# A fused attention and expert kernel: two routing tables for three, wide head sums, an earlier first image, and a new order of work

## The chip, the cores and the metric

One core of a Trainium2 chip runs the whole program in one launch. The metric is the device time of one execution in microseconds (us). Times inside the program are counted from its first instruction. The engines have names of their own in what follows: TensorE (PE, and PEld for its weight loads), VectorE (DVE), ScalarE (ACT), GpSimd (POOL) and SyncE (SP), which here only issues transfers.

## The reference, cut to what matters

Eight images of 128 channels and 256 positions go through three layers; T = 2 halves of 128 positions make an image.

```python
# 1. per image: self-attention over positions, with a key mask
sim = softmax((wq x + bq)^T (wk x + bk) / 8 + key_mask);  x = x + gamma * (sim @ (wv x))
# 2. t = tokens of x.  L = 256, but the sequence axis of this layer is the 8 images:
q, k = relu(LN(t) @ q_w.T + q_b), relu(LN(t) @ k_w.T + k_b);  v = LN(t) @ v_w.T + v_b
q_, k_ = [q*sin, q*cos], [k*sin, k*cos]              # angle by the position in the sequence
attn = (q_ @ cumsum(k_ v)) / max(q_ @ cumsum(k_), eps)   # causal, 8 heads of 16
t = t + attn @ out_w.T + out_b
# 3. mixture of 8 experts, the best 2 per token
probs = softmax(LN(t) @ router_w); w, e = top_k(probs, 2); w = w / w.sum()
t = t + sum over the 2 of  w * (silu(x @ w1[e]) * (x @ w3[e])) @ w2[e]
```

The causal sum over images is written out: for image i and every earlier or equal image j, the product of q(i) and k(j), summed within each head and times the cosine of the gap i - j, is the weight of v(j).

## The kernel before, in words

Each engine runs a list of steps, written out by hand in its own order; semaphores tie them together. The lists are the long rows of calls at the end of each engine's function. A step is a small function with the same name on every engine's side of the work, and its number is the image or the block.

- **Conv layer** (`conv_...`, per image): projections (L646, L647, L653), scores (L661), row maxima on VectorE (L899), exponentials on ACT (L529), turns by TensorE (L671), the product with the values (L681).
- **Linear layer** (`lin_...`, per image i): a norm whose root is taken on GpSimd (L455), projections (L698, L699, L705), products q(i) k(j) for all j <= i on VectorE (L951), the **head sums** on TensorE in `lin_scores` (L720): the product is the stationary operand, and a [128, 8] slice of the constants (the cosine in the rows of each head) is the moving one, so that every matmul moves 8 columns. Then VectorE weights (L974), values (L989), turns that add over j (L733) and the output projection `lin_out` (L743, L744). Images from the third on have products and values in two halves.
- **Routing** (`route_...`, per image): norm, logits (L758), the two best, ranks by triangular matmuls (L770 to L776), a slot for each of the token's two rows. GpSimd scatters rows with four indirect DMAs per image (L474) into `rows_x` in DRAM, where each expert has room for all tokens. `rows_x` is first filled with blank rows from the tile `pad` by nine large DMAs on SyncE's queue (L411, L413).
- **Tables.** The 39 blocks of 128 rows are not known before routing. A table says for each block where its rows start and which expert it has. `PHASES` (L37) says when tables are made: after 4 images for 9 blocks, after 6 images for blocks up to 17, after all 8 for the rest. A table takes `count` and `t_turn` on TensorE and some ten small steps (`t_...`) on VectorE. SyncE waits for the table and for the scatters of its images before it loads the rows of its blocks (L418, L424).
- **Expert blocks.** Per block s: `turn_x` (L795), its copy on ACT (L584), `gate_up` (L809, four f32 matmuls, eight instructions), silu on ACT (L590), `hidden` on VectorE (L1183), `down` (L820), `weigh` (L1204), `store`, an indirect DMA of GpSimd into `rows_y` (L483). The weights of the expert are copied into a ring of three, by ACT (`weights`, L602) for blocks before the last table, by VectorE (L1194) for those of it.
- **End.** When all stores have landed, `rows_y` is read back in six parts, added to the tokens (L1265, L1267) and written out.

The queue of SyncE is in order: image 0 (X), WC, VEC, CF, XT of image 0, small constants, X and XT of the other images, the expert weights W13 and W2, then the blank fill. The first conv projection waits for both transfers of its image (L644), since they count on one semaphore. GpSimd clears `pad` first. The stores and the scatters share GpSimd's list: stores 0 to 3 stand before the scatters of images 6 and 7.

Of the kernel before, what the change touches and what calls it, by code (L numbers as in the profile page):

```python
# [15 lines left out]
P = 128  # L16
B = 8
# [5 lines left out]
H = 8  # L23
# [13 lines left out]
PHASES = ((4, 9), (6, 17), (B, BLOCKS),)  # L37
# [60 lines left out]
def hybrid_block(nc, x_ch, x_tok, w_conv, w_lin, w_router, w13, w2, vecs, bias_rows, cst_f, cst_tri, cst_dest,  # L98
                 out):
    ctx = ExitStack()  # L100
    with ctx:
# [15 lines left out]
        W13 = sb("W13", [P, E * 2 * F])  # L117
        W2 = sb("W2", [P, E * FK * P])
# [44 lines left out]
        num = sb("num", [P, 2, B, T * P])  # L163
        attT = sb("attT", [P, 2, N])
# [34 lines left out]
        pad = sb("pad", [P, CAP // P, ROW])  # L199
# [47 lines left out]
        ld_x = [sem(f"ld_x{i}") for i in range(B)]  # L247
        ld_vec = sem("ld_vec")
# [34 lines left out]
        qk_done = sem("qk_done")  # L283
        sc_done = sem("sc_done")
# [106 lines left out]
        def _(sp):  # L391
            sp.dma_start(X[:, 0, :], x_ch[:, 0, :]).then_inc(ld_x[0], 16)
            sp.dma_start(WC[:, :], w_conv).then_inc(ld_conv, 16)
            sp.dma_start(VEC[:, :], vecs).then_inc(ld_vec, 16)
            sp.dma_start(CF[:, :], cst_f).then_inc(ld_cst, 16)
            sp.dma_start(XT[:, 0, :, :], x_tok[:, 0, :, :]).then_inc(ld_x[0], 16)
# [16 lines left out]
            sp.dma_start(rows_x[DUMMY:DUMMY + P, :], pad[:, 0, :]).then_inc(rows_blank, 16)  # L413

# [27 lines left out]
        def _(pool):  # L442

            pool.memset(pad[:, :, 0:DEST_COL], 0.0).then_inc(pad_ready, 1)
            pool.memset(pad[:, :, DEST_COL:ROW].bitcast(I32), SKIP).then_inc(pad_ready, 1)
            pool.wait_ge(ld_dest, 16)
# [40 lines left out]
            rstd_lin(0); rstd_lin(1); rstd_lin(2); rstd_ffn(0); rstd_ffn(1); rstd_lin(3); rstd_lin(4); scatter(0, 0)  # L487
            scatter(0, 1); scatter(0, 2); scatter(0, 3); rstd_ffn(2); rstd_lin(5); scatter(1, 0); scatter(1, 1)
            scatter(1, 2); scatter(1, 3); rstd_lin(6); rstd_ffn(3); rstd_lin(7); scatter(2, 0); scatter(2, 1)
            scatter(2, 2); scatter(2, 3); scatter(3, 0); scatter(3, 1); scatter(3, 2); scatter(3, 3); rstd_ffn(4)  # L490
            rstd_ffn(5); scatter(4, 0); scatter(4, 1); scatter(4, 2); scatter(4, 3); rstd_ffn(6); scatter(5, 0)
            scatter(5, 1); scatter(5, 2); scatter(5, 3); store(0); rstd_ffn(7); store(1); store(2); store(3)
            scatter(6, 0); scatter(6, 1); scatter(6, 2); scatter(6, 3); scatter(7, 0); scatter(7, 1); scatter(7, 2)
            scatter(7, 3)
            for s in range(4, BLOCKS):
                store(s)

        @block.scalar
        def _(act):

            act.wait_ge(ld_vec, 16)
# [126 lines left out]
            for s in range(16, 38):  # L628
                turn_and_silu(s)

        @block.tensor
        def _(pe):
# [76 lines left out]
            def lin_scores(i, share):  # L709
# [5 lines left out]
                if share == 0:  # L715
                    bank_free(BANK_SC, sco_done, i + 1)
# [141 lines left out]
            for s in range(13, BLOCKS + 1):  # L858
                block_step(s)
# [454 lines left out]
```

## Time and profile before

| what | value |
|---|---|
| median of 3 runs | 211.65 us (210.78 to 212.57) |
| the profiled execution | 212.31 us, of which its span is 210.2 us |
| PE busy | 161.9 us, 77% of the span |
| PE weight loads | 148.7 us, 71% |
| DVE busy | 117.7 us, 56% |
| ACT busy | 75.7 us, 36% |
| POOL busy | 89.5 us, 43% |
| mean granted clock of TensorE | 0.875 |

### The profile page before, as it was taken

Reading aid. Unit: us, or ns where it says so; the run is one execution under the profiler, and the core shown is the slowest. Engines: PE = TensorE matmul, PEld = TensorE weight load, DVE = VectorE, ACT = ScalarE, POOL = GpSimd, SP = SyncE. Lnnn points to the kernel's source line nnn. Section 1 sums busy time; section 2 is a strip of 40 time slices with the busy share of each in tenths; the row PEclk is TensorE's granted clock in tenths of the full one; section 3 lists DMA queues with packets and bytes.
Section 4 is the critical chain, followed back from the end, with each engine's and each line's share of the span. In section 5 each row is a group of like instructions: output and inputs, shape, how many; then the busy total and the mean of one; then the engine's idle time right before and its main releaser. Section 6 shows DMA issues by size and latency. Waiting matters only on the chain.

```text
span 210.2 us, 4168 instructions
## 1 busy us (share of the span) xinstructions
PE 161.9 (77%) x1161; PEld 148.7 (71%) x1161; DVE 117.7 (56%) x475; ACT 75.7 (36%) x227; POOL 89.5 (43%) x94
## 2 busy tenths in 40 slices
PE   0998999999499998899997885731999899992000
PEld 0677888989499887799996875731999888881000
DVE  0525566888559888655453853412465555553154
ACT  2256767563471530021451553304242333330000
POOL 4001111215862267502756543774476556657000
PEclk9999999999969998555589699996699999999555
DMA  5789999950110001113101024111443220110395
GB/s 127 213 257 382 427 420 411 422 224 13 40 54 0 0 28 41 38 30 87 38 26 54 22 69 102 41 50 37 101 112 107 71 73 21 35 47 0 111 278 210
DMA packets 15475, 25.33 MB, mean 121 GB/s; under 512 B 3083, under 2 KB 13008, under 8 KB 14174
## 3 DMA queue, kind: packets, MB, share of 16 engines
q1 hardware_dynamic: 13182, 20.84, 29.7%
q0 software_dynamic: 2272, 4.24, 6.2%
q8 instruction: 10, 0.16, 0.3%
q14 instruction: 11, 0.09, 0.1%
HBM read 10.67 MB, written 14.85 MB: 121 GB/s over the span
## 4 chain that ended last, share of the span: by engine, by line
PE 67%; another core or an unknown queue 8%; issue 5%; DMA 5%; ACT 5%; DVE 3%; SPq 2%; POOL 1%; POOLq 1%; ACTq 1%; DVEq 0%
PE ps L809 18%; PE ps L720 7%; PE ps L820 7%; PE ps L733 5%; PE ps L681 4%; PE ps L661 4%; PE ps L743 3%; DMA num<-rows_y 3%; PE ps L795 2%; PE ps L671 2%; PE ps L698 2%; PE ps L699 2%; PE ps L646 2%; PE ps L705 2%
## 5 line engine op out<-in xcount | busy, mean ns | idle before, releaser
L483 POOL DMA_INDIRECT rows_y<-yb,xb x39 | 39.5, 1012 | 23.7 <-DVE yb L1204 14.7
L809 PE MATMUL ps<-xbT,WB 128*128 128x128 f32 x312 | 46.5, 297 | 2.5 <-issue 2.4
L809 PEld LDWEIGHTS ps<-xbT,WB 128*128 128x128 f32 x312 | 42.4, 211 | 3.8 <-issue 3.8
L474 POOL DMA_INDIRECT rows_x<-xrow,slot x32 | 34.3, 1071 | 24.2 <-DVE slot L1085 16.2
L1204 DVE TENSOR_SCALAR yb<-ps,xb 128x128 f32<-128x128 f32 x39 | 13.6, 348 | 39.3 <-PE ps L820 23.5
L590 ACT ACTIVATE gate<-ps 128x256 f32<-128x256 f32 x39 | 14.9, 384 | 41.2 <-PE ps L809 28.7
L820 PE MATMUL ps<-W,hid 128*128 x156 | 25.0, 285 | 1.1 <-DVE hid L1183 1.1
L795 PE MATMUL ps<-CF,xb 128*128 128x128 f32 x39 | 11.8, 303 | 14.4 <-ACT xbT L584 11.2
L820 PEld LDWEIGHTS ps<-W,hid 128*128 128x128 f32 x156 | 21.4, 199 | 1.7 <-issue 1.5
L720 PEld LDWEIGHTS ps<-CF,qk 128*128 128x128 f32 x144 | 20.4, 223 | 0.2
L720 PE MATMUL ps<-CF,qk 128*128 128x8 f32 x144 | 20.4, 275 | 0.0
L455 POOL TENSOR_TENSOR rs<-ve,CF 128x2 f32<-128x2 f32 x8 | 6.7, 843 | 28.9 <-DVE ve L933 28.9
L795 PEld LDWEIGHTS ps<-CF,xb 128*128 128x128 f32 x39 | 6.3, 160 | 15.4 <-issue 15.2
L1183 DVE TENSOR_TENSOR hid<-gate,ps 128x256 f32<-128x256 f32 x39 | 16.1, 412 | 1.0 <-ACT gate L590 1.0
L461 POOL TENSOR_TENSOR rs<-ve,CF 128x2 f32<-128x2 f32 x8 | 6.6, 826 | 22.4 <-DVE ve L1015 21.9
L584 ACT ACTIVATE xbT<-ps 128x128 f32<-128x128 f32 x39 | 10.8, 278 | 13.3 <-PE ps L795 6.1
L733 PE MATMUL ps<-CF,num 128*128 128x128 f32 x72 | 14.0, 350 | 0.9 <-DVE num L989 0.9
L951 DVE TENSOR_TENSOR qk<-kT,qT 128x768 f32<-128x768 f32 (+3 forms) x13 | 11.6, 892 | 2.1 <-ACT kT L549 1.7
L733 PEld LDWEIGHTS ps<-CF,num 128*128 128x128 f32 x72 | 11.5, 185 | 1.8 <-DVE num L989 0.9
L989 DVE TENSOR_TENSOR num<-vt,sco 128x768 f32<-128x768 f32 (+3 forms) x13 | 11.6, 891 | 0.5 <-DVE sco L974 0.3
L602 ACT ACTIVATE WB<-W 128x512 f32 x17 | 10.6, 626 | 2.6 <-DVE table L1160 2.0
L681 PE MATMUL ps<-cv,probT 128*128 128x128 f32 x64 | 8.8, 281 | 2.8 <-ACT cv L520 2.8
(128 smaller groups left out, 286.9 us busy)
## 6 DMA issues: line engine op xcount, KB each, us to landing
rows_x<-pad SPq DMA_DIRECT2D x8, 1105.0 KB, 21.5
xb<-rows_x SPq DMA_DIRECT2D x39, 65.0 KB, 1.9
W<-in_w SPq DMA_DIRECT2D x1, 2048.0 KB, 10.3
num<-rows_y SPq DMA_DIRECT2D x8, 192.0 KB, 4.6
X<-in_x_ch SPq DMA_DIRECT2D x8, 128.0 KB, 3.2
XT<-in_x_tok SPq DMA_DIRECT2D x8, 128.0 KB, 3.6
W<-in_w SPq DMA_DIRECT2D x1, 1024.0 KB, 12.2
out_tok<-num SPq DMA_DIRECT2D x4, 192.0 KB, 3.6
```

Source lines behind the costliest of these rows:

```text
L474: pool.indirect_dma_start(rows_x, bass.IndirectOffsetOnAxis(ap=slot[:, g:g + 1], axis=0), xrow[:, g // TOP_K, g % TOP_K, :], None, bounds_ ...
L483: pool.indirect_dma_start(rows_y, bass.IndirectOffsetOnAxis(ap=xb[:, n, DEST_COL:ROW].bitcast(I32), axis=0), yb[:, n, :], None, bounds_che ...
L590: act.activation(gate[:, s % GATE, :], ps_gu[s % 3][:, 0:F], ACT.Silu).then_inc(gate_done, 1)
L681: last = pe.matmul(ps_co[:, t, :], probT[:, b, k, t * P:(t + 1) * P], cv[:, b, k, :], start=(k == 0), stop=(k == T - 1))
L720: last = pe.matmul(ps_sc[:, j, t * H:(t + 1) * H], qk[:, i % 2, j, t * P:(t + 1) * P], heads, start=True, stop=True)
L733: last = pe.matmul(ps_aT[:, t * P:(t + 1) * P], num[:, i % 2, j, t * P:(t + 1) * P], ident, start=(j == 0 and t == 0), stop=(j == i), is_t ...
L795: pe.transpose(bank(xbT_bank(s))[:, 0:P], xb[:, s % RING, 0:P], ident).then_inc(xbT_done, 1)
L809: last = pe.matmul(ps_gu[s % 3][:, k * P:(k + 1) * P], WB[:, s % WBS, k * P:(k + 1) * P], xbT[:, s % XBT, :], start=True, stop=True)
L820: last = pe.matmul(ps_yb[s % 2], hid[:, s % HID, k * P:(k + 1) * P], W2[:, bass.ds(experts[s] * (FK * P) + k * P, P)], start=(k == 0), sto ...
L951: dv.tensor_tensor(qk[:, i % 2, first:end, :], kT[:, first:end, :], qT[:, i % 2, :].unsqueeze(1).broadcast_to([P, end - first, N]), ALU.mult)\
L1183: dv.tensor_tensor(hid[:, s % HID, :], gate[:, s % GATE, :], ps_gu[s % 3][:, F:2 * F], ALU.mult)\
L1204: dv.tensor_scalar(yb[:, n, :], ps_yb[s % 2], xb[:, n, W_COL:W_COL + 1], None, ALU.mult).then_inc(yb_done, 1)
```

## The change

`PHASES` becomes two tables: 13 blocks after 5 images, and the other 26 after all 8. ACT copies the weights of blocks 0 to 12 and VectorE those of 13 to 38.

The head sums get a moving operand of 128 columns. `HZ` holds, for every gap, the 8 cosine columns with zeros on both sides; a slice of it puts the 8 columns where image j and half t have theirs, and all matmuls of an image add up in the same 128 columns of PSUM.

The weights of the conv layer and VEC are issued by ACT. XT of image 0 gets a semaphore of its own. The expert weights come behind the blank fill and wait for it, since `pad` is now a view of the first 2,210 columns of W13. GpSimd also clears HZ and copies the cosines into it. TensorE starts with 22 bf16 matmuls of 128 columns on the tile ONES. The lists of all engines are in a new order; on GpSimd all scatters now stand before the first store.

```diff
-PHASES = ((4, 9), (6, 17), (B, BLOCKS),)
+PHASES = ((5, 13), (B, BLOCKS),)
...
+        pad = W13[:, 0:CAP // P * ROW].rearrange("p (k d) -> p k d", d=ROW)
+        HZ = sb("HZ", [P, B, (2 * B * T - 1) * H])
-        pad = sb("pad", [P, CAP // P, ROW])
...
             sp.dma_start(X[:, 0, :], x_ch[:, 0, :]).then_inc(ld_x[0], 16)
-            sp.dma_start(WC[:, :], w_conv).then_inc(ld_conv, 16)
-            sp.dma_start(VEC[:, :], vecs).then_inc(ld_vec, 16)
             sp.dma_start(CF[:, :], cst_f).then_inc(ld_cst, 16)
-            sp.dma_start(XT[:, 0, :, :], x_tok[:, 0, :, :]).then_inc(ld_x[0], 16)
+            sp.dma_start(XT[:, 0, :, :], x_tok[:, 0, :, :]).then_inc(ld_xt0, 16)
...
-            sp.dma_start(W13[:, :], w13).then_inc(ld_w13, 16)
-            sp.dma_start(W2[:, :], w2).then_inc(ld_w13, 16)
 
             sp.wait_ge(pad_ready, 2)
...
             sp.dma_start(rows_x[DUMMY:DUMMY + P, :], pad[:, 0, :]).then_inc(rows_blank, 16)
+
+            sp.wait_ge(rows_blank, 16 * (E + 1))
+            sp.dma_start(W13[:, :], w13).then_inc(ld_w13, 16)
+            sp.dma_start(W2[:, :], w2).then_inc(ld_w13, 16)
...
             pool.memset(pad[:, :, DEST_COL:ROW].bitcast(I32), SKIP).then_inc(pad_ready, 1)
+            pool.memset(HZ[:, :, :], 0.0).then_inc(heads_ready, 1)
+            pool.wait_ge(heads_ready, 1)
+            pool.wait_ge(ld_cst, 16)
+            pool.tensor_copy(HZ[:, :, (B * T - 1) * H:B * T * H],
+                             CF[:, C_COS:C_COS + B * H].rearrange("p (g h) -> p g h", g=B)).then_inc(heads_ready, 1)
...
-            scatter(5, 1); scatter(5, 2); scatter(5, 3); store(0); rstd_ffn(7); store(1); store(2); store(3)
-            scatter(6, 0); scatter(6, 1); scatter(6, 2); scatter(6, 3); scatter(7, 0); scatter(7, 1); scatter(7, 2)
-            scatter(7, 3)
-            for s in range(4, BLOCKS):
+            rstd_ffn(7); scatter(5, 0); scatter(5, 1); scatter(5, 2); scatter(5, 3); scatter(6, 0); scatter(6, 1)
+            scatter(6, 2); scatter(6, 3); scatter(7, 0); scatter(7, 1); scatter(7, 2); scatter(7, 3)
+            for s in range(0, BLOCKS):
                 store(s)
...
+            act.dma_start(WC[:, :], w_conv).then_inc(ld_conv, 16)
+            act.dma_start(VEC[:, :], vecs).then_inc(ld_vec, 16)
             act.wait_ge(ld_vec, 16)
...
+            def warm_up():
+
+                pe.wait_ge(dve, 1)
+                for _ in range(22):
+                    pe.matmul(ps_aT[:, 0:P], ONES[:, :], ONES[:, :], start=True, stop=True)
+
             def conv_proj_qk(i):
...
-                pe.wait_ge(ld_x[i], 32)
+                pe.wait_ge(ld_x[i], 32 if i else 16)
...
+                if i == 0:
+                    pe.wait_ge(heads_ready, 2)
                 for j in range(first, end):
-                    heads = CF[:, C_COS + (i - j) * H:C_COS + (i - j + 1) * H]
                     for t in range(T):
-                        last = pe.matmul(ps_sc[:, j, t * H:(t + 1) * H], qk[:, i % 2, j, t * P:(t + 1) * P], heads,
-                                         start=True, stop=True)
+                        at = (B * T - 1 - (j * T + t)) * H
+                        last = pe.matmul(ps_sc, qk[:, i % 2, j, t * P:(t + 1) * P], HZ[:, i - j, at:at + B * T * H],
+                                         start=(j == 0 and t == 0), stop=(j == i and t == T - 1), skip_group_check=True)
...
+            lin_proj_v(7); lin_out_turn(5, 0); route_turn(4); lin_scores(6, 0); route_logits(4); lin_scores(6, 1)
+            lin_out_turn(5, 1); lin_out(5); route_rank(4); count(0); lin_scores(7, 0); lin_scores(7, 1)
+            lin_out_turn(6, 0); lin_out_turn(6, 1); t_turn(0); lin_out(6); lin_out_turn(7, 0); route_turn(5)
+            route_logits(5); lin_out_turn(7, 1); turn_x(0); lin_out(7); turn_x(1); gate_up(0); turn_x(2); gate_up(1)
+            route_rank(5); route_turn(6); turn_x(3); gate_up(2); route_logits(6); down(0); route_turn(7); turn_x(4)
+            gate_up(3); down(1); route_rank(6); turn_x(5); gate_up(4); down(2); turn_x(6); route_logits(7)
+            gate_up(5); down(3); turn_x(7); gate_up(6); down(4); route_rank(7); count(1); turn_x(8); gate_up(7)
+            down(5); turn_x(9); gate_up(8); down(6); turn_x(10); t_turn(1); gate_up(9); down(7)
+            for s in range(9, BLOCKS + 1):
                 block_step(s)
...
-            dv.memset(ONES[:, :], 1.0)
+            link(dv.memset(ONES[:, :], 1.0))
...
-                dv.wait_ge(ld_x[i], 32)
+                dv.wait_ge(ld_xt0, 16) if i == 0 else dv.wait_ge(ld_x[i], 32)
```

## Rows read from the trace of the kernel before

**Rows 1.** Page: TensorE's granted clock in tenths, 40 equal slices.

```profile
PEclk9999999999969998555589699996699999999555
```

**Rows 2.** Stretches: length, busy us (instructions) by engine, granted clock, DMA share, GB/s.

```profile
0.00:14.20 14.20, 8.77 (x26) 6.32 (x27) 4.08 (x18) 5.29 (x13) 2.56 (x7) 1.00 0.74 197
14.20:58.60 44.40, 40.57 (x303) 36.15 (x302) 30.87 (x139) 26.41 (x80) 12.46 (x15) 1.00 0.71 286
58.60:62.00 3.40, 3.40 (x16) 3.12 (x15) 2.57 (x9) 2.24 (x5) 2.79 (x3) 0.51 0.15 44
62.00:82.50 20.50, 19.56 (x172) 18.51 (x171) 17.27 (x72) 6.83 (x21) 8.65 (x10) 1.00 0.06 18
82.50:106.40 23.90, 22.90 (x113) 21.56 (x112) 14.72 (x66) 5.78 (x18) 10.69 (x10) 0.50 0.18 48
106.40:116.60 10.20, 7.85 (x74) 7.42 (x73) 4.36 (x21) 3.96 (x12) 5.40 (x6) 1.00 0.11 34
116.60:120.00 3.40, 3.40 (x18) 3.40 (x18) 3.13 (x25) 2.10 (x7) 2.55 (x3) 0.51 0.07 22
120.00:143.90 23.90, 14.04 (x122) 12.74 (x121) 7.98 (x40) 7.99 (x23) 14.66 (x16) 1.00 0.24 65
143.90:150.70 6.80, 4.38 (x21) 4.41 (x22) 2.07 (x8) 1.90 (x6) 2.73 (x4) 0.50 0.22 56
150.70:188.50 37.80, 35.22 (x303) 33.78 (x303) 22.60 (x66) 12.59 (x44) 23.15 (x23) 1.00 0.26 69
```

**Rows 3.** Order of time, start: start us, us, engine, operation, idle before.

```profile
0.82 0.17 DVE L872 MEMSET ONES<- 65x128 bf16 x1 [0.82 <-PEq L1306]
...
5.20 1.09 PE L646 MATMUL ps<-X,WC 128*65 128x256 f32 x2 [5.20 <-DMA XT<-in_x_tok]
```

**Rows 4.** Chain that ended last: start us, us on the chain, what.

```profile
2.58 2.48 DMA XT<-in_x_tok
...
23.43 0.43 PE ps L699 x2
...
70.79 1.24 PE ps L720 x12
...
155.95 0.89 PE ps L809 x8
```

**Rows 5.** Order of time, around two holes, one long sum, one slow block.

```profile
57.13 1.13 PE L681 MATMUL ps<-cv,probT 128*128 128x128 f32 x8 [2.76 <-ACT cv L520]
...
78.65 3.27 PE L720 MATMUL ps<-CF,qk 128*128 128x8 f32 x28
...
133.82 1.06 PE L809 MATMUL ps<-xbT,WB 128*128 128x128 f32 x8
...
142.32 0.38 ACT L590 ACTIVATE gate<-ps 128x256 f32<-128x256 f32 x1 [4.73 <-remote]
...
145.87 0.35 DVE L1204 TENSOR_SCALAR yb<-ps,xb 128x128 f32<-128x128 f32 x1 [8.61 <-remote]
...
146.32 0.45 PE L795 MATMUL ps<-CF,xb 128*128 128x128 f32 x1 [6.58 <-ACT xbT L584]
...
149.14 0.42 PE L795 MATMUL ps<-CF,xb 128*128 128x128 f32 x1
```

**Rows 6.** Order of time, GpSimd: first and last of six stores back to back.

```profile
136.64 0.97 POOL L483 DMA_INDIRECT rows_y<-yb,xb  x1 [0.31 <-issue]
...
143.02 0.97 POOL L483 DMA_INDIRECT rows_y<-yb,xb  x1 [0.30 <-issue]
```

**Rows 7.** Groups by line: operation, shapes, count, busy us, mean ns, idle before.

```profile
L444 POOL MEMSET pad<- 128x2193 f32 x1 | 1.9, 1927 | 0.3 <-POOLq L1306 0.3
...
L706 PEld LDWEIGHTS ps<-BIAS,ONES 65*128 65x128 bf16 x16 | 1.6, 100 | 0.0
```

**Rows 8.** Stretches, line L809 alone: length, PE and PEld busy (instructions), clock, DMA.

```profile
82.50:106.40 23.90, 3.83 (x16) 3.69 (x16) 0.50 0.18 48
...
150.70:190.80 40.10, 25.09 (x187) 22.49 (x186) 1.00 0.25 67
```

More of the change, by code:

```diff
@@ L283, in hybrid_block @@
         qk_done = sem("qk_done")
+        heads_ready = sem("heads_ready")
         sc_done = sem("sc_done")
@@ new lines, in _ @@
+            turned_x(2); silu(1); route_xT(6); weights(4); turned_x(3); silu(2); weights(5); turned_x(4)
+            route_xT(7); route_lean(6); silu(3); weights(6); turned_x(5); silu(4); weights(7); turned_x(6); silu(5)
+            weights(8); route_lean(7); turned_x(7); silu(6); weights(9); turned_x(8); silu(7); weights(10)
+            turned_x(9); silu(8); weights(11); turned_x(10); silu(9); weights(12); turned_x(11); silu(10)
+            turned_x(12); silu(11); turned_x(13); silu(12)
+            for s in range(12, 38):
@@ L857, in _ @@
-            down(9); turn_x(13); gate_up(12); down(10); turn_x(14); gate_up(13); t_turn(2); down(11)
-            for s in range(13, BLOCKS + 1):
+            conv_scores(1); conv_out(0); conv_proj_qk(2); conv_proj_v(2); conv_turn(1); conv_scores(2); conv_out(1)
+            lin_turn(0); conv_proj_qk(3); conv_proj_v(3); lin_proj_qk(0); lin_proj_v(0); conv_turn(2)
+            conv_scores(3); lin_turn(1); lin_scores(0, 0); conv_out(2); lin_proj_qk(1); conv_turn(3); conv_proj_v(4)
+            lin_out_turn(0, 0); lin_proj_v(1); conv_proj_qk(4); lin_scores(1, 0); lin_out(0); lin_turn(2)
@@ L1258, in _ @@
-            weigh(12); hidden(14); weights(17); weigh(13); hidden(15)
-            for s in range(15, BLOCKS + 1):
+            conv_max(0); conv_inverse(0); conv_max(1); conv_add(0); lin_stats(0); conv_inverse(1); lin_moments(0)
+            lin_eps(0); lin_norm(0); conv_max(2); conv_add(1); lin_stats(1); conv_inverse(2); lin_moments(1)
+            lin_eps(1); lin_norm(1); lin_products(0, 0); conv_max(3); lin_sum(0); lin_floor(0); lin_inverse(0)
+            lin_weights(0); conv_add(2); conv_inverse(3); lin_values(0, 0); lin_stats(2); lin_moments(2)
@@ new lines, in _ @@
+            route_slots(6); weigh(2); hidden(4); route_top(7); route_index(7); route_gap(7); route_mask(7)
+            route_seen(7); weigh(3); hidden(5); route_weights(7); weigh(4); route_where(7); t_blocks(1)
+            route_slots(7); hidden(6); t_sum(1); t_ends(1); t_delta(1); t_past(1); weigh(5); t_skip(1); hidden(7)
+            t_expert(1); t_row(1); weigh(6); hidden(8); t_read(1); weigh(7); hidden(9); weigh(8); hidden(10)
+            weights(13); weigh(9); hidden(11)
+            for s in range(11, BLOCKS + 1):
```

142 lines of the change are left out of this document (57 added, 85 removed).

## The prediction

> **What bounds the kernel now.** I read the page first, then one table of stretches cut where the granted clock changes, then the order of time in the stretches that look odd. The page has TensorE as the busiest engine, and its clock line dips [rows 1]. The table of stretches is the main view [rows 2]. Up to 58.6 us TensorE is nearly full (40.57 us busy of 44.4) and is the bound. From 62 to 82.5 it is full and VectorE nearly so (17.27 of 20.5). From 82.5 to 106.4 the granted clock is 0.50: TensorE is busy for 22.90 of 23.9 us, but at the lower level, 1.2 GHz, so it is the bound only because of its clock; VectorE has 14.72 us of work there. From 106.4 to 150.7 nothing is full: TensorE is busy for 29.67 us of 44.3, 7.8 us of that at the lower level. From 150.7 to 188.5 TensorE is full again (35.22 of 37.8) with the expert blocks alone, and 21.7 us follow it: last blocks, last stores, sum, output.
>
> Two things in these views matter. The first 14 us: the page grants 1.00 there, but two 256-column matmuls take 1.09 us at 5.2 us [rows 3] and 0.43 us later [rows 4], so the array runs at 1.2 GHz at first, whatever the clock column says. And the holes after 106.4: gate_up(12) is done at 134.88, yet the silu that waits for it starts at 142.32, and VectorE, which waits for a `down` from before that, at 145.87; TensorE meanwhile stands still for 6.58 us [rows 5]. In that time GpSimd runs indirect stores back to back, one per 1.28 us [rows 6]. Neither ACT nor VectorE has another reason to wait, so signals of TensorE seem to arrive late while GpSimd has a backlog. A smaller hole of this kind is the 2.76 us before 57.13 [rows 5].
>
> **The sum, part by part**, against the profiled execution: span 210.2 us, 212.3 us with what lies around it, 0.3% above the median of 211.65 us.
>
> Start. The first matmul waits until 5.20 us for the second transfer of image 0 (XT), which only VectorE needs [rows 3]. The change gives it a semaphore of its own and issues WC and VEC from ACT's queue, so TensorE could start once X and WC are there; XT's own transfer took 2.48 us [rows 4], X and WC are issued by 1.2 us now, so about 3.6 us. In front of it are now 22 warm-up matmuls, from about 1 us on, when ONES is set [rows 3]. Their price is not in the trace: 22 weight loads of 100 ns [rows 7] (2.2 us) from below, and half more for a slow clock; the first real matmul then starts at 4.4 us. That saves 0.8 us (between a loss of 1.3 and a gain of 1.6). The clock: 8.77 us of work lie before 14.2 us, all slow [rows 2]. If it rises some 4.4 us sooner, that work shrinks by 2.2 us; bounds 0 and 4.4. ACT's two DMA issues go ahead of a table load and cost nothing that waits. **Start: -3.0 us.**
>
> GpSimd. HZ is cleared: 1984 columns at the rate of 2193 in 1.93 us [rows 7], 1.75 us, plus a small copy. GpSimd is busy for 2.56 of the first 14.2 us [rows 2], so 0. `pad` is set before it, so the fill of rows does not wait for it.
>
> SyncE's queue. Two issues leave its front and two of weights leave the place before the fill, which so comes four issues sooner, without 3 MB ahead of it. The weights now wait for the whole fill, SyncE with them; behind it on that queue are only row loads, far later. The first weights are wanted near 90 us, and the queues are quiet long before (a DMA share of 0.06 from 62 to 82.5 [rows 2]). **0.**
>
> Stretch 14.2 to 62. It is TensorE's own work. The dip at 58.6 (3.40 us busy, slow) follows the 2.76 us hole. I take half of the hole's chance: -1.0 for it, -1.7 for the dip. **-2.7 us**, bounds 0 and -4.5. So what stood at 62 stands at 56.3.
>
> Head sums. Two matmul instructions per pair of image and half, 144 in all, now move 128 columns instead of 8. Twelve 8-column ones take 1.24 us, 103 ns each; 128-column ones of the same type take 0.89/8 = 111 ns [rows 4]. The weight load behind each sets the pace, so the columns are nearly free: 144 x 8 ns = +1.2 us while TensorE is the bound. The column price if nothing hid it: a 256-column one takes 0.43/2 = 215 ns, 104 ns more for 128 columns, so 120 columns x 144 is at most +14 us.
> The Trainium skill (TensorE: Matmul & The Clock Gate, Back-to-back issue gap) lets the gap follow the moving columns down to a floor of about 25 ns, 56 ns for 128; by it alone the widening would cost 31 ns x 144 = 4.5 us and the time would be about 195. The rows disagree: 8 columns take 103 ns here.
>
> Stretch 62 to 106.4 (44.4 us). The clock falls at 82.5, right behind a run of 28 matmuls of 8 columns [rows 5]. If wide sums hold it at 2.4 GHz, TensorE's work of the linear stage is 19.56 + (22.90 - 5.4)/2 = 28.3 us, +1 for the sums; the 5.4 are two expert blocks' gate-and-up (3.83 [rows 8]) and some 1.6 of turns. VectorE's is 17.27 + 14.72 = 32.0 us and barely shrinks. VectorE becomes the bound, at 95%: 34 us. **-10.4 us.** So the point that was 106.4 is at 90.3, and lin_out(7), the last matmul of this stage, ends 2.5 us later, at 93. It has done no expert block yet, where the kernel before had done two.
>
> First table, 13 blocks, and the routing of images 5 to 7 among them. TensorE needs 1.62 us per block (37.8 us, 187/8 = 23.4 blocks [rows 2, 8]) plus some 3.5 us of routing: 25 us without a hole. The kernel before did 39 - 2 - 23.4 = 13.6 blocks between 106.4 and 150.7, 44.3 us; without its own 2.5 us of lin_out, 41 for 13. One table less takes away one place where everything waits for routing, and all of images 5 to 7 are routed while the 13 blocks run; but twelve indirect stores of rows now follow one another on GpSimd, with all 39 of the block outputs behind them, and such runs went with the holes. I leave 6 of the 16 us: **31 us, to 124**.
>
> Second table: 26 blocks x 1.62 = 42 us, +1 for the first rows to land: **43 us, to 167**. ACT no longer copies weights in them, VectorE does for 26 instead of 22; 22.60 us busy in 37.8 leave room [rows 2]. GpSimd: the last scatter ends near 116, and 39 stores at 1.28 us end at 166, with the last block. No term of its own, but no slack either.
>
> End as before: **21.7 us** [rows 2], so span 188.7, and with the 2.1 around it **191 us**.
>
> **Rivals.**
> A, the forecast: the clock holds in the linear stage, holes stay in part. 191 us, own range 184 to 198. Chance 0.42.
> B, the clock falls again in the linear stage, because waits on VectorE or the transposes between the sums let it. Then the -10.4 is lost: 201 us. For it: VectorE is the bound there, so TensorE will pause. Against: the stretch from 14.2 to 58.6, with many transposes, is granted 1.00 throughout [rows 2]. Chance 0.20.
> C, the holes stay at full size, because GpSimd's row of 12 scatters and a backlog of 13 stores makes them. The 13 blocks take 41 us: 201; if the backlog also stops the first blocks of the second table, as six stores stopped TensorE for 6.58 us, 207. Self-limiting, since GpSimd runs dry when no block ends. Chance 0.17.
> D, the holes go entirely: 185, with VectorE denser 180. Chance 0.10.
> E, slower: holes in the second table send the clock to 1.2 GHz and it stays there. A slow block takes 149.14 - 146.32 = 2.82 us [rows 5], 1.2 more than a fast one. From 19 of the 26 on the kernel is slower than before; all 26 give 191 + 31 = 222. For it: two such dips stand after holes. Against: both ended after 3.4 and 6.8 us [rows 2]. Chance 0.07.
> F, the sums cost their columns: 191 + 14 = 205. Chance 0.04.
>
> **The numbers.** About 1% can be told from no change here. The likeliest case gives 191. The range reaches from D's near end into C: 181 to 206, leaving out E, the far end of C and of D. Faster by over 1%: A, B, D, F and nearly all of C, 0.89, less 0.03 for several losses together: 0.86. Within 1%: 0.05. Slower: E and such sums, 0.09.
>
> **What would show it.** Start: first real matmul near 4.4 us, fast ones well before 14. Linear stage: granted clock 1.00 where it is 0.50 from 82.5 on, L720's mean no higher than 300 ns, VectorE over 90% busy, last lin_out near 93 us. First table: 13 blocks in about 31 us, with the longest idle times of TensorE before a transpose of rows, released by ACT. Second table: 1.62 us per block; GpSimd's stores without a pause. I am wrong if the granted clock falls among the wide sums, or if the stretch of the second table costs over 2 us per block.

## The result: 200.46 us, faster by 5.7%; and the profile after

The changed kernel takes 200.46 us (median of 4 runs, 198.63 to 202.54) against 211.22 us of the kernel before (4 runs, 210.31 to 212.57). The ratio is 0.943, with a 95% interval of 0.934 to 0.951. (Ratios, here and below, compare undisturbed runs alone and so may differ from the quotient of two medians.) I had forecast 191 us with a range of 181 to 206: the sign and the range held, but of the 20.7 us that I had expected only 10.8 came.

The profiled execution of the changed kernel is one of its longest, 202.54 us with a span of 200.4. So the sums below, which are made against that span, show some 2 us more than a typical execution has.

The page's row of the granted clock, 40 equal slices:

```profile
PEclk9999999999999999996698899855999999998555
```

The long low stretch of [rows 1], slices 17 to 20 (82.5 to 106.4 us in [rows 2]), is gone. What is left are dips behind 91 us. The table of stretches, cut where the clock changes; columns as in [rows 2]:

```profile
0.00:13.00 13.00, 11.46 (x48) 8.75 (x49) 4.05 (x18) 5.42 (x13) 4.32 (x9) 1.00 0.74 211
13.00:56.00 43.00, 41.32 (x314) 37.24 (x313) 33.40 (x147) 26.20 (x79) 14.94 (x17) 1.00 0.76 301
56.00:75.00 19.00, 17.23 (x145) 15.88 (x145) 16.24 (x69) 8.84 (x26) 9.68 (x11) 1.00 0.06 19
75.00:91.50 16.50, 13.95 (x124) 12.73 (x122) 14.34 (x52) 3.32 (x11) 10.80 (x8) 1.00 0.09 30
91.50:98.30 6.80, 6.28 (x28) 5.76 (x29) 3.81 (x21) 1.74 (x7) 0.69 (x1) 0.50 0.47 107
98.30:108.50 10.20, 8.20 (x81) 7.97 (x80) 5.61 (x32) 6.23 (x19) 4.79 (x6) 1.00 0.15 43
108.50:112.00 3.50, 3.50 (x19) 3.50 (x18) 1.51 (x9) 1.36 (x5) 2.77 (x3) 0.52 0.13 40
112.00:129.00 17.00, 8.99 (x78) 8.12 (x76) 4.42 (x22) 4.38 (x12) 11.28 (x12) 1.00 0.21 63
129.00:139.30 10.30, 5.86 (x27) 5.89 (x28) 3.28 (x10) 2.04 (x7) 4.78 (x5) 0.50 0.33 84
139.30:179.00 39.70, 37.60 (x318) 35.62 (x317) 24.15 (x71) 13.54 (x47) 25.41 (x24) 1.00 0.21 59
```

TensorE is nearly full up to 56 us (41.32 us busy of the 43 behind the first 13) and from 139.3 to 179 (37.60 of 39.70). Between 112 and 129 us it is busy for 9 us of 17, while GpSimd (fifth pair) works for 11.28. The order of time at the longest hole, TensorE, ACT, VectorE and GpSimd, with the idle time before in brackets:

```profile
118.91 0.27 PE L811 MATMUL ps<-CF,xb 128*128 128x128 f32 x1
119.02 1.06 PE L825 MATMUL ps<-xbT,WB 128*128 128x128 f32 x8
...
120.75 0.97 POOL L491 DMA_INDIRECT rows_y<-yb,xb  x1 [0.30 <-issue]
121.44 0.35 DVE L1219 TENSOR_SCALAR yb<-ps,xb 128x128 f32<-128x128 f32 x1 [3.45 <-PE ps L836]
...
122.84 0.28 ACT L593 ACTIVATE xbT<-ps 128x128 f32<-128x128 f32 x1 [1.97 <-remote]
...
123.40 1.12 PE L825 MATMUL ps<-xbT,WB 128*128 128x128 f32 x8
...
129.68 0.97 POOL L491 DMA_INDIRECT rows_y<-yb,xb  x1 [0.30 <-issue]
132.79 0.38 ACT L599 ACTIVATE gate<-ps 128x256 f32<-128x256 f32 x1 [9.67 <-remote]
132.85 0.35 DVE L1219 TENSOR_SCALAR yb<-ps,xb 128x128 f32<-128x128 f32 x1 [10.74 <-remote]
...
133.44 2.05 PE L825 MATMUL ps<-xbT,WB 128*128 128x128 f32 x8 [8.37 <-issue]
133.48 0.97 POOL L491 DMA_INDIRECT rows_y<-yb,xb  x1 [2.83 <-DVE yb L1219]
```

This is [rows 5] and [rows 6] again. TensorE finishes gate_up(10) at 120.1, but the silu that waits for it starts at 132.79, and VectorE gets its `down` at 132.85. Both engines are released within 0.06 us of one another, 2.1 us after GpSimd has ended a run of unbroken indirect DMAs (scatters from 115.65, stores from 120.75 to 130.65). The run does not stop every signal: at 121.44 VectorE and at 122.84 ACT still get results of TensorE, the second 3.7 us after the matmul at 118.91 had ended; then nothing comes through for 9.7 us. In [rows 5] it is alike: the silu at 142.32 starts inside GpSimd's run, VectorE at 145.87 behind it.

### The profile page after: what moved, and what is told of

Read it like the earlier page. It is cut to its first block, busy times and chain, and to the rows that moved or that the text cites. A ratio compares the mean times of both kernels' runs of the same rounds, so it can differ in the third digit from the quotient of the medians.

```text
span 200.4 us, 4191 instructions
## 1 busy us (share of the span) xinstructions
PE 156.5 (78%) x1181; PEld 143.2 (71%) x1181; DVE 118.8 (59%) x464; ACT 73.7 (37%) x223; POOL 93.4 (47%) x96
## 3 DMA queue, kind: packets, MB, share of 16 engines
q0 software_dynamic: 2272, 4.24, 6.4%
## 4 chain that ended last, share of the span: by engine, by line
PE 66%; issue 11%; DMA 5%; ACT 5%; DVE 4%; POOL 3%; SPq 2%; POOLq 1%; another core or an unknown queue 0%; ACTq 0%
PE ps L825 20%; PE ps L836 9%; PE ps L736 6%; PE ps L675 4%; PE ps L749 3%; PE ps L695 3%; PE ps L811 2%; DMA num<-rows_y 2%; PE ps L759 2%; POOL rows_x L482 2%; PE ps L685 2%; PE ps L774 2%; PE ps L712 2%; PE ps L719 2%; PE ps L660 2%
## 5 line engine op out<-in xcount | busy, mean ns | idle before, releaser
L491 POOL DMA_INDIRECT rows_y<-yb,xb x39 | 40.6, 1040 | 24.4 <-DVE yb L1219 16.2
L825 PEld LDWEIGHTS ps<-xbT,WB 128*128 128x128 f32 x312 | 41.6, 207 | 12.5 <-issue 11.7
L482 POOL DMA_INDIRECT rows_x<-xrow,slot x32 | 36.5, 1140 | 23.2 <-DVE slot L1100 15.6
L1219 DVE TENSOR_SCALAR yb<-ps,xb 128x128 f32<-128x128 f32 x39 | 13.6, 348 | 41.2 <-PE ps L836 29.2
L736 PE MATMUL ps<-HZ,qk 128*128 128x128 f32 x144 | 18.4, 278 | 0.0
L463 POOL TENSOR_TENSOR rs<-ve,CF 128x2 f32<-128x2 f32 x8 | 5.7, 708 | 26.6 <-DVE ve L948 26.6
L736 PEld LDWEIGHTS ps<-HZ,qk 128*128 128x128 f32 x144 | 17.1, 192 | 0.1
L469 POOL TENSOR_TENSOR rs<-ve,CF 128x2 f32<-128x2 f32 x8 | 6.4, 797 | 14.9 <-DVE ve L1030 14.7
L1209 DVE COPY WB<-W 128x512 f32 x26 | 11.2, 430 | 0.8 <-issue 0.8
L749 PE MATMUL ps<-CF,num 128*128 128x128 f32 x72 | 10.8, 290 | 0.3 <-DVE num L1004 0.3
L538 ACT ACTIVATE prob<-ps,nmax 128x256 f32<-128x256 f32 x16 | 7.4, 469 | 6.3 <-DVE nmax L914 6.2
L675 PE MATMUL ps<-ck,cq 65*128 65x256 f32 x32 | 9.6, 427 | 0.1
```

Of the source, the lines that this page charges most:

```text
L482: pool.indirect_dma_start(rows_x, bass.IndirectOffsetOnAxis(ap=slot[:, g:g + 1], axis=0), xrow[:, g // TOP_K, g % TOP_K, :], None, bounds_ ...
L491: pool.indirect_dma_start(rows_y, bass.IndirectOffsetOnAxis(ap=xb[:, n, DEST_COL:ROW].bitcast(I32), axis=0), yb[:, n, :], None, bounds_che ...
L675: last = pe.matmul(ps_sim[:, t, :], cq[:, b, t * P:(t + 1) * P], ck[:, b, :], start=True, stop=True)
L736: last = pe.matmul(ps_sc, qk[:, i % 2, j, t * P:(t + 1) * P], HZ[:, i - j, at:at + B * T * H], start=(j == 0 and t == 0), stop=(j == i and ...
L749: last = pe.matmul(ps_aT[:, t * P:(t + 1) * P], num[:, i % 2, j, t * P:(t + 1) * P], ident, start=(j == 0 and t == 0), stop=(j == i), is_t ...
L825: last = pe.matmul(ps_gu[s % 3][:, k * P:(k + 1) * P], WB[:, s % WBS, k * P:(k + 1) * P], xbT[:, s % XBT, :], start=True, stop=True)
```

## The ledger of the sum

| stretch | forecast us | measured us |
|---|---|---|
| start to the end of the last `lin_out` | 93 | 96.5 |
| from there to gate_up(13): the 13 blocks and the routing | 31 | 39.9 |
| second table, to 179.0 | 43 | 42.7 |
| end | 21.7 | 21.4 |
| span | 188.7 | 200.4 |

In the kernel before, the last `lin_out`, that of image 7, stands among the expert blocks:

```profile
110.62 0.22 PE L744 MATMUL ps<-BIAS,ONES 65*128 65x128 bf16 x1
```

So the two kernels are better compared at the blocks. gate_up(0) starts at 101.95 us before and at 96.60 now, gate_up(15), behind the holes of both, at 149.35 and at 140.67. The change gains 5.4 us up to the first block, 3.3 us from there to gate_up(15), where the old order still has linear work of image 7 to do (turns and `lin_out`, some 3 us), and 1.1 us behind it. Two terms of the sum are off: the way to the last `lin_out` by 3.5 us, the first table by 8.9 us. The experiments ask what each part of the change is worth, and what makes the 39.9 us.

## Experiments: what each part is worth

Theory 1 is mine: the wide sums hold the clock in the linear stage, and that is most of the gain. Its rival: the new order and the earlier start hold it.

**a1_narrow**, the changed kernel with narrow sums:

```
+  heads = CF[:, C_COS + (i - j) * H:C_COS + (i - j + 1) * H]
...
-  last = pe.matmul(ps_sc, qk[...], HZ[:, i - j, at:at + B * T * H], start=(j == 0 and t == 0), ...)
+  last = pe.matmul(ps_sc[:, j, t * H:(t + 1) * H], qk[...], heads, start=True, stop=True)
```

> The changed kernel with the head sums as they were, 8 moving columns each; the clear of HZ and the order stay. If the wide sums are what holds TensorE's clock at 2.4 GHz in the linear stage, the granted clock falls to 0.50 somewhere between 60 and 91 us, as it did at 82.5 us in the kernel before, and 6 to 11 us come back: 206 to 211 us. If the new order of work or the earlier start holds it, the clock stays at 1.00 there and the time stays at 199 to 202 us, or falls by the 1.2 us that I had put down for the columns.

**b1_wide**, the kernel before with wide sums:

```
+  HZ = sb("HZ", [P, B, (2 * B * T - 1) * H])          (cleared by GpSimd, moving operand as in the change)
-  pad = sb("pad", [P, CAP // P, ROW])
+  pad = W13[:, 0:CAP // P * ROW]...                   (W13, W2 loaded behind the fill)
...
```

> The kernel before with the wide head sums alone (and with the blank rows in W13's place and W13, W2 loaded behind the fill, since HZ has no room otherwise). If the wide sums hold the clock, the granted clock is 1.00 from 82.5 to 106.4 us where it was 0.50, and the -10.4 us of that stretch appear nearly whole: 200 to 203 us. If the rest of the linear stage lets the clock fall anyway, or if VectorE had been the bound all along, 209 to 212 us. If the moving columns cost their time, up to 225 us.

Measured: a1_narrow 206.45 us (205.52 to 211.61), ratio to the kernel before 0.986 (0.965 to 1.008). So by the medians 6.0 us of the 10.8 are back with this one change; by the two ratios (0.986 against 0.943) it is 9 us, and their intervals allow 3 to 15. b1_wide 204.88 us (203.88 to 205.18), 7.7 us below the median of the kernel before beside it (212.57); its ratio, 0.979 (0.970 to 0.989), makes that only 4.4 us (2.4 to 6.4). So each is a gain of some us, not a sharp number. The order of time in a1_narrow, where its clock falls first:

```profile
54.54 1.49 PE L736 MATMUL ps<-CF,qk 128*128 128x8 f32 x12
...
61.23 1.06 PE L712 MATMUL ps<-xnT,WL 128*128 128x256 f32 x2
```

The stretch from 82.5 to 106.4 us of b1_wide (columns of [rows 2]), and then a run of 28 wide sums, in order of time; [rows 5] has the 28 narrow ones of the same place, at 78.65 us:

```profile
82.50:106.40 23.90, 19.27 (x173) 17.74 (x172) 18.07 (x83) 8.29 (x26) 14.08 (x14) 1.00 0.20 55
```

```profile
78.78 3.37 PE L731 MATMUL ps<-HZ,qk 128*128 128x128 f32 x28
```

Two projections of 256 columns take 1.06 us at 61.23, where the same view has 0.59 us for such a pair at 14.47 us in the changed kernel (shown below): the clock is low there, some us behind 12 narrow sums. From 80 to 95 us, with narrow sums again, a1_narrow is granted 0.54. In b1_wide it is granted 1.00 in the very stretch where [rows 2] has 0.50, with 173 matmuls done instead of 113. And 28 wide sums take 3.37 us where 28 narrow ones took 3.27. b1_wide also moves the weight loads and clears HZ; a1_narrow leaves both as they are, and the two agree. Theory 1 stands for the clock. Its price was too high: I had put 10.4 us on it, the two runs show 6 and 7.7 by their medians, 9 and 4.4 by their ratios.

**a2_nowarm** leaves `warm_up()` out of TensorE's list.

> The changed kernel without the 22 warm-up matmuls. If they bring the fast clock sooner, the first conv matmul starts at about 3.1 us instead of 3.84, but matmuls stay slow for about a microsecond or more longer, until 14 us and later: 200.5 to 203 us. If the moment at which matmuls become fast does not depend on them, they only delay the first matmul by 0.7 us: 199 to 200.5 us.

**b2_start** puts the change's start into the kernel before: `ld_xt0`, WC and VEC issued by ACT, and `warm_up()`.

> The kernel before with the change's start alone: a semaphore of its own for XT of image 0, WC and VEC issued by ACT, the warm-up matmuls. First real matmul at 3.8 us where it stood at 5.20. If that time is kept up to the end: -1.4 us, 209 to 210.5 us; if the fast clock comes some 4 us sooner as well: -3 us, 208 us; if a later wait (the dip of the clock at 82.5 us, which may come earlier as well) takes it back: 211 to 212 us.

**b3_wide_start** joins b1_wide and b2_start.

> The kernel before with wide sums and the change's start together; three tables and the old order stay. Wide sums alone gave 7.7 us (b1_wide, 204.88), the start alone 0 to 2.7 us. If the two add up and the rest of the change (tables, order, place of the stores) is worth what is left of the 10.8 us: 202 to 204 us, so 2 to 3 us for the rest. If the holes take the start's time back: 204 to 206. If tables and order are worth nothing: 200 to 201 us.

Measured: a2_nowarm 201.04 us, ratio 0.957 (0.938 to 0.977); b2_start 209.83 us, ratio 1.0005 (0.991 to 1.010); b3_wide_start 201.28 us (199.31 to 203.88), beside 210.33 us of the kernel before on that chip (204.34 to 213.60, too scattered for a ratio with an interval). The start alone is worth nothing that can be told. a2_nowarm lies in its first case by the number, but 0.6 us from the changed kernel's 200.46 is no difference, and its profile fits neither case. With start and sums the kernel before comes within 1 us of the changed one, within 3 us if the medians of each chip are compared (0.957 against 0.943). That is all that is left for tables, order and the place of the stores together, and with no interval here it can't be told from nothing.

The order of time at the start, first of the changed kernel and then of a2_nowarm:

```profile
3.84 1.12 PE L660 MATMUL ps<-X,WC 128*65 128x256 f32 x2 [0.27 <-DMA WC<-in_w_conv]
...
9.45 1.06 PE L661 MATMUL ps<-X,WC 128*65 128x256 f32 x2
...
14.47 0.59 PE L660 MATMUL ps<-X,WC 128*65 128x256 f32 x2
```

```profile
3.94 1.12 PE L660 MATMUL ps<-X,WC 128*65 128x256 f32 x2 [3.94 <-DMA WC<-in_w_conv]
...
8.46 0.65 PE L660 MATMUL ps<-X,WC 128*65 128x256 f32 x2 [0.22 <-DMA XT<-in_x_tok]
```

The first conv matmul waits for WC with or without the warm-up, so here the warm-up costs nothing. But it does not bring the fast clock either: without it a pair of 256 columns is fast at 8.46 us (0.65 us), with it still slow at 9.45 (1.06 us).

**h4_rstd** moves one wait: TensorE's clock falls at 91.5, right behind an idle time of 1.21 us in front of route_turn(5), which waits for a root that GpSimd takes only behind four scatters. In the changed kernel:

```profile
90.84 0.44 PE L767 MATMUL ps<-CF,xrow 128*128 128x128 f32 x2 [1.21 <-DVE xrow L1036]
```

```
- scatter(4, 0); scatter(4, 1); scatter(4, 2); scatter(4, 3); rstd_ffn(5); rstd_ffn(6)
+ scatter(4, 0); rstd_ffn(5); scatter(4, 1); scatter(4, 2); scatter(4, 3); rstd_ffn(6)
```

> The changed kernel with GpSimd's rstd_ffn(5) right behind scatter(4, 0) instead of behind scatter(4, 3), and rstd_ffn(6) behind scatter(4, 3) as it was. In the profile rs of image 5 starts at 89.28 us, TensorE then waits 1.21 us in front of route_turn(5) and its clock falls at 91.5 us for 6.8 us (6.28 us of slow work, 3.1 us lost). If that wait lets the clock fall: rs starts at 86.1 us, no dip at 91.5, 3 to 5 us less, 195 to 198 us. If the time saved goes into the holes behind 105 us: 199 to 201 us.

Measured: 201.62 us (201.39 to 202.08), ratio 0.953 (0.945 to 0.962): nothing gained, and just above both of its ranges. From 90 to 95 us TensorE is busy for 2.15 us of 5, and the clock dips all the same. The wait went to another place: the idle time before route_turn(5) is gone, and at 93.47 us TensorE has stood 2.85 us for the first rows of a block (`xb<-rows_x`). These rows also wait for the last scatter of image 4, which ends at 90.14 us in h4_rstd and at 89.26 in the changed kernel.

## Experiments: what makes the holes

Theory H: while GpSimd runs indirect DMAs back to back, TensorE's completion signals are held back. Theory Q: something in TensorE's own queue or in the tables makes them.

**h1_direct**: SyncE stores the outputs of blocks 0 to 7 as plain transfers into a spare tensor. They leave the result incomplete: those rows stay zero in it, since `rows_y` is cleared beforehand (2 MB behind the fill). So its time is that of a kernel that leaves eight blocks out of the result.

```
+  for s in range(8):                                            (SyncE, behind the row loads of table 0)
+      sp.wait_ge(yb_done, s + 1)
+      sp.dma_start(rows_z[s * P:(s + 1) * P, :], yb[:, s, :]).then_inc(easy_stored, 16)
...
-  for s in range(0, BLOCKS): store(s)
+  for s in range(8, BLOCKS): store(s)
```

> The changed kernel, with the outputs of blocks 0 to 7 stored by SyncE as plain transfers into a spare tensor (their rows so stay zero in the result: rows_y is cleared beforehand, 2 MB behind the fill of rows). GpSimd then has its 12 scatters after 100 us and only stores from block 8 on: the unbroken run of 12 indirect DMAs from 115.65 to 130.65 us shrinks to 4 scatters. Theory H (TensorE's completion signals are held back while GpSimd runs indirect DMAs back to back, and come through when it pauses): the idle time of 8.37 us before L825 and the 2.73 us before it go, and the dip of the clock behind them, 9 to 12 us in all: 188 to 192 us. Theory Q (the wait is in TensorE's own queue or in the new table, whoever stores): a hole of 6 us or more stays between 118 and 134 us and the time is 199 to 201 us. Theory L (a hole of another place follows at once, since the rows of the second table are late): 194 to 198 us.

**h2_between**: two stores in front of the scatters of image 6, two in front of those of image 7.

```
- scatter(5, 3); scatter(6, 0) ... scatter(6, 3); scatter(7, 0) ... scatter(7, 3); store(0) ...
+ scatter(5, 3); store(0); store(1); scatter(6, 0) ... scatter(6, 3); store(2); store(3); scatter(7, 0) ... store(4) ...
```

> The changed kernel with stores 0 and 1 moved in front of the scatters of image 6 and stores 2 and 3 in front of those of image 7, where GpSimd idles 2.6 and 2.5 us for their slots. The run that ends at 130.65 us has 8 indirect DMAs instead of 12, but the pauses between the runs go. Theory H as a rule of unbroken runs: one long run from 100.9 to about 126 us, so the hole comes sooner and is as long: 198 to 204 us. If only the length of the backlog behind the last scatter counts, it is 4 stores (5.1 us) shorter: 194 to 197 us.

**h3_paced**: a pause behind 20 of the indirect DMAs.

```
+  def pause():
+      pool.memset(rest[:, :], 0.0).then_inc(rest_done, 1)       (512 columns)
+      paused[0] += 1
+      pool.wait_ge(rest_done, paused[0])
```

> The changed kernel with a pause of GpSimd (a memset of 512 columns into a spare tile, and the wait for it, some 0.5 to 1 us) behind each scatter of images 5 to 7 and behind each of the first 8 stores: 20 pauses, 10 to 20 us of GpSimd's time. Theory H: signals come through in the pauses, as they do in the second table, where a store starts each 1.6 us: no idle time of TensorE over 3 us behind 100 us, clock 1.00 there, 190 to 195 us, or 196 to 199 if the later end of the stores (about 6 us behind the last block) takes part of it. Theory Q: holes stay, and the pauses come on top: 203 to 212 us.

**p1_short** and **p2_stores** use the same pause with 16 columns: p1 at the same 20 places, p2 behind stores 0 to 11 only.

> As h3_paced, with the pause cut to a memset of 16 columns and the wait for it. In h3_paced the 13 blocks of the first table ran without a hole, and then TensorE stood 14.06 us for the rows of the second, since GpSimd's 12 scatters had taken 2.31 us each; with the short pause I expect about 1.85 us each and the last scatter near 119 us. If a short pause lets TensorE's signals through as well: no idle time of TensorE over 2 us before 113 us, then one of some 8 us for rows, 197 to 201 us. If it takes the longer pause, holes come back between 100 and 113 us and the rows are late as well: 202 to 208 us.

> The changed kernel with the short pause behind stores 0 to 11 only; the scatters run unbroken as they did. If pauses among the stores are enough to let TensorE's signals through: the holes up to 115 us stay, the 8.37 us before L825 shrink to 3 us or less, and the time is 193 to 197 us. If the pause of 0.1 us is too short among stores, which leave only 0.28 us behind it: the hole stays at 8 us or grows with the run by a microsecond or two, 200 to 203 us.

Measured: h1_direct 189.59 us (189.34 to 190.57), ratio 0.896 (0.887 to 0.904); h2_between 198.24 us (197.37 to 198.71), ratio 0.935 (0.926 to 0.945); h3_paced 207.27 us (205.60 to 210.23); p1_short 200.19 us (197.73 to 202.80); p2_stores 199.25 us (197.96 to 200.38).

The times alone: h1_direct is where Theory H put it; h2_between lies at the near edge of what H gives for unbroken runs (198 to 204) and misses the 194 to 197 of a shorter backlog; h3_paced is as slow as Theory Q said; p1_short fits a short pause that is long enough; p2_stores lies between its cases. So the times don't decide, and the traces must.

h1_direct takes away the long hole. What is left in the first table are idle times of 2.67 us before 104.29 and of 2.03 us before 119.42, each behind four scatters in a row, and the two dips of its clock row stand there (slices 23 and 24, and slightly 26 and 27):

```profile
PEclk9999999999999999999999579889999999997555
```

h3_paced is the decisive view, although it is slow. TensorE and GpSimd in order of time: first block, last `down` before the wait for rows, that wait, the hole behind the pauses, and GpSimd from its first scatter of image 5 on:

```profile
93.50 1.91 PE L839 MATMUL ps<-xbT,WB 128*128 128x128 f32 x8
...
113.22 0.61 PE L850 MATMUL ps<-W,hid 128*128 x4
127.89 0.47 PE L825 MATMUL ps<-CF,xb 128*128 128x128 f32 x1 [14.06 <-DMA xb<-rows_x]
...
154.82 2.05 PE L839 MATMUL ps<-xbT,WB 128*128 128x128 f32 x8 [8.29 <-issue]
```

```profile
97.81 1.04 POOL L485 DMA_INDIRECT rows_x<-xrow,slot  x1 [0.39 <-issue]
...
121.21 0.97 POOL L485 DMA_INDIRECT rows_x<-xrow,slot  x1 [0.80 <-POOL rest L494]
...
123.52 0.97 POOL L485 DMA_INDIRECT rows_x<-xrow,slot  x1 [0.80 <-POOL rest L494]
...
127.09 0.97 POOL L501 DMA_INDIRECT rows_y<-yb,xb  x1 [0.28 <-POOL rest L494]
...
142.78 0.97 POOL L501 DMA_INDIRECT rows_y<-yb,xb  x1 [0.30 <-issue]
...
188.26 0.97 POOL L501 DMA_INDIRECT rows_y<-yb,xb  x1 [0.30 <-issue]
```

With a scatter each 2.31 us, the way from gate_up(0) to the end of down(9), which holds 12 `gate_up`, 10 `down` and the routing among them, takes 20.3 us (93.50 to 113.83) with no idle time over 0.31 us. The changed kernel takes 28.4 us for the same steps (96.60 to 124.96), with two idle times of 2.00 and 2.73 us and two dips of the clock, and its 8.37 us follow. (The expectation of p1_short speaks of 13 blocks without a hole in h3_paced; these are the steps it means.) Then TensorE stands 14.06 us for rows that the slow scatters have not yet written. While the stores are paced (1.79 us each, 125 to 141) there is no hole; the pauses end at 141, stores follow one another each 1.27 us, and a hole of 8.29 us is there. One program thus has holes where GpSimd runs unbroken and none where it pauses. (The pause is itself 0.55 us of work of GpSimd, so it is not a busy GpSimd as such that does it.) Theory Q had put holes into the paced stretches.

How long must the pause be? p1_short, the same view:

```profile
101.97 0.97 POOL L485 DMA_INDIRECT rows_x<-xrow,slot  x1 [0.80 <-issue]
103.86 0.97 POOL L485 DMA_INDIRECT rows_x<-xrow,slot  x1 [0.80 <-issue]
...
123.65 0.97 POOL L501 DMA_INDIRECT rows_y<-yb,xb  x1 [0.28 <-POOL rest L494]
125.03 0.97 POOL L501 DMA_INDIRECT rows_y<-yb,xb  x1 [0.28 <-POOL rest L494]
```

```profile
125.25 0.48 PE L825 MATMUL ps<-CF,xb 128*128 128x128 f32 x1 [9.75 <-DMA xb<-rows_x]
135.55 2.05 PE L839 MATMUL ps<-xbT,WB 128*128 128x128 f32 x8 [4.24 <-issue]
```

Scatters each 1.89 us: no hole up to 115 us, then 9.75 us of waiting for rows. Stores each 1.38 us: a hole of 4.24 us. In p2_stores, with the same 1.38 us, one of 5.36 us stays. So 0.8 us between the end of one indirect DMA and the start of the next is enough (the paced stores of h3_paced), 0.4 us is not, and 0.3 us, which is what the queue leaves by itself, is not either. The length of the run counts too: behind 150 us the changed kernel's stores come in threes, 1.27 to 1.48 us apart, with 1.1 us or more of idle time between the groups, and TensorE has no idle time over 1 us there up to 180; four scatters in a row go with 2.00 us, twelve DMAs with 8.37.

**v1_early**, the last run, adds an earlier routing of image 5 to h2_between (TensorE: `route_rank(5)` behind `lin_out(7)`; VectorE: `route_where(5)` and `route_slots(5)` in front of the first `hidden`; GpSimd: `scatter(5, 0)` in front of `rstd_ffn(7)`).

> As h2_between (198.24 us), with the routing of image 5 finished sooner: route_rank(5) right behind lin_out(7) on TensorE, route_where(5) and route_slots(5) in front of the first hidden on VectorE, scatter(5, 0) in front of rstd_ffn(7) on GpSimd. Theory G (from the first scatter of image 5 on, the 51 indirect DMAs that are left on GpSimd set the end, at some 1.6 us each with the pauses that TensorE needs): the first of them starts 1 to 3 us sooner (97.49 us in h2_between) and all that follows with it: 195.5 to 197.5 us. Theory T (TensorE's own work in that stretch sets the end, GpSimd only makes it wait here and there): the rank of image 5 in front of the first block changes nothing, 198 to 199 us, or 200 if TensorE then waits in front of its first block.

Measured: 197.65 us (197.11 to 200.31), ratio 0.938 (0.930 to 0.946). Beside h2_between's 0.935 it is no difference, and the first scatter starts at 98.49 us in its profile, not sooner. So it tells nothing on its two theories. h2_between and v1_early both lie below the changed kernel's 0.943, but the intervals overlap: a gain of about 1% that is likely, not shown.

## Why moving holes gains nothing

Here are GpSimd's first scatter of image 5 and its last store, in the changed kernel, in h2_between and in p1_short; 51 indirect DMAs stand from the one to the other in each:

```profile
100.90 1.04 POOL L482 DMA_INDIRECT rows_x<-xrow,slot  x1 [0.39 <-issue]
...
184.40 0.97 POOL L491 DMA_INDIRECT rows_y<-yb,xb  x1 [0.30 <-issue]
```

```profile
97.49 1.03 POOL L482 DMA_INDIRECT rows_x<-xrow,slot  x1 [0.38 <-issue]
...
179.69 0.97 POOL L491 DMA_INDIRECT rows_y<-yb,xb  x1 [0.30 <-issue]
```

```profile
99.99 1.04 POOL L485 DMA_INDIRECT rows_x<-xrow,slot  x1 [0.39 <-issue]
...
182.71 0.97 POOL L501 DMA_INDIRECT rows_y<-yb,xb  x1 [0.30 <-issue]
```

The distances are 83.5, 82.2 and 82.7 us, 1.64 to 1.67 us for each of the 50 steps, and the span ends 16 to 17 us behind the last store in all three. Unbroken, a step takes 1.27 us. This average has two parts. In the second table TensorE itself is the bound: it is busy for 37.60 us of 39.70, a block takes 42.7 / 26 = 1.64 us, and the stores wait for the blocks.

In front of that, from the first scatter of image 5 to store(12), stand 24 steps of GpSimd. They take 40.5 us in the changed kernel (100.90 to 141.39), 39.0 in h2_between, 40.2 in p1_short and 41.4 in the kernel before: 1.63 to 1.73 us a step, wherever the holes lie. GpSimd either runs at 1.27 us and stops TensorE, until no block is finished and it runs dry, or it leaves pauses and TensorE runs. h3_paced, with the long pauses, takes 47.5 us. h1_direct has 16 steps there and takes 31.5 us (97.31 to 128.80), 9 us less: that is most of its gain (last store at 171.67, span 188.4). That this pair of engines is the bound in that stretch is worked out from these distances. h1_direct, the one run that takes indirect DMAs away, goes that way, but it changes the issuing engine and the kind of transfer at once; fewer indirect DMAs for a whole result were not tried.

## Why the prediction was right, and short

1. **Start, -3.0 us: wrong in size.** The first real matmul was forecast at 4.4 us and came at 3.84. The 2.2 us for an earlier fast clock did not come: matmuls are slow up to 12 us, as before up to 14. (The forecast set 1.09 us from the order of time beside 0.43 us from the chain; in the order of time a fast pair takes 0.59 us. That the first ones are slow holds in either view.) b2_start's ratio of 1.0005 says that what is left did not reach the end.
2. **Queues, clear of HZ, the place of W13: 0, right as far as seen.** b1_wide has all three and is faster.
3. **Head sums, +1.2 us, at most 14: right.** 28 of them take 3.37 us wide (b1_wide) and 3.27 us narrow ([rows 5]), both at the fast clock; over 144 sums that is 0.5 us. Rival F is out. The 4.5 us that the forecast worked out by the formula of the Trainium skill (TensorE: Matmul & The Clock Gate, Back-to-back issue gap) are not seen either. That section gives the formula for an isolated matmul, and says that in a stream where each matmul has its weight load both set the spacing, which fits what is seen here.
4. **Linear stage, -10.4 us: the mechanism is right, the sum too high** (4.4 to 9 us by the runs' ratios). The clock holds up to 91.5 us; the wide sums do it, as a1_narrow and b1_wide show from both sides. But VectorE was busy for 30.6 us of the 35.5 from 56 to 91.5, 86% and not 95%, with routing steps that waited for roots taken behind scatters (1.21 us of TensorE's idle time before route_turn(5)); and the clock fell once for 6.8 us at 91.5, a small part of rival B. The last `lin_out` ended at 96.5, not 93.
5. **First table, 31 us: this is the step that failed.** It took 39.9 us. I put 25 us of work and 6 us of holes into it, so I gave 10 of the 16 us of holes back, because one table less takes a waiting place away. They stayed: TensorE's idle times of over 1 us between the first block and gate_up(15) are 2.00, 2.73 and 8.37 us, 13.1 in all; in the kernel before they are 6.58 us [rows 5] and these three, 13.6 in all:

```profile
116.35 0.30 PE L795 MATMUL ps<-CF,xb 128*128 128x128 f32 x1 [2.21 <-ACT xbT L584]
...
130.72 0.30 PE L795 MATMUL ps<-CF,xb 128*128 128x128 f32 x1 [2.42 <-ACT xbT L584]
...
137.74 0.30 PE L795 MATMUL ps<-CF,xb 128*128 128x128 f32 x1 [2.42 <-issue]
```

   b3_wide_start leaves 1 us for tables and order together by the medians, 3 us if each chip's own kernel before is taken. The holes go with GpSimd's runs, not with the table, and the change left all its indirect DMAs in place and put them into longer runs. That was rival C's mechanism ("GpSimd's row of 12 scatters and a backlog of 13 stores makes them") and rival C's number, 41. I had given it 0.17; [rows 5] and [rows 6] had shown the cause before, and the only evidence against it was an argument on tables.
6. **Second table 43 us, end 21.7 us: right** (42.7 and 21.4). Rival E did not occur: the clock is at 1.00 from 139.3 to 179.

So the time is that of rival C (201), with most of forecast A's linear stage. The range held because it reached into C, not because the forecast's own sum was right.

## What to carry to other kernels

When two engines that wait for a third are released at the same instant, long after it was done, look for what a fourth was doing without a pause: here GpSimd's indirect DMAs. Count the indirect DMAs in the stretch where the others need it, times the pace that leaves room for them (24 times some 1.65 us here). If that is as long as the stretch, moving waits about or taking a table out gains nothing that can be told; only fewer such DMAs there, or another queue for them, has shortened it here. And look at what the granted clock does behind runs of short matmuls: here it fell to 0.50 among sums of 8 columns and stayed at 1.00 through those of 128, which cost 0.1 us in 28 sums.

## What the hardware showed that I had not expected

- TensorE's finished work became visible to ACT and VectorE late, by up to 12.7 us (gate_up(10) ends at 120.1, silu at 132.79), while GpSimd ran indirect DMAs back to back: in runs of four and more at 1.27 us and in a run at 1.38 us per DMA, not at 1.79, 1.89 or 2.31 us. Some signals came inside such runs, at the start of one on time, then late; the last ones came 1.8 to 2.2 us behind the run's end in the changed kernel and in h3_paced. What holds the signals is open. No run here looks inside. The Trainium skill (DMA: Bandwidth & Descriptors, SWDGE vs HWDGE vs iDMA) says that GpSimd computes each descriptor itself and appends it to rings in SBUF, while SyncE's are made in hardware; h1_direct, where SyncE issues eight of the stores, agrees with a difference between the two paths, and no more than that: its stores are plain as well.
- 22 warm-up matmuls from 1.04 us on did not raise the clock sooner, and the kernel without them had fast matmuls 4 us earlier (8.46 us against 12.4 us at the earliest; 13.7 us in the kernel before), while the page grants 1.00 in both from the start. This is one profile without them and two with them (b2_start has the same times), so a difference by chance is not excluded.
